# A four-layer residual stack on one core: the set-up work behind the RNN's first 64 steps, laid out anew

## The reference

```python
x = x + L0(x, h0=cond)        # RNN: h = tanh(x_t @ Wx + b + h @ Wh), 1024 steps
x = x + L1(x, conv_w=cond)    # 4-tap convolution, @ Wp and @ Ws, softplus, tanh, state scan, @ Wo
x = x + L2(x, h0=cond)        # LSTM, 512 wide, 1024 steps
x = x + L3(x, ada_emb=cond)   # x @ (base + x_a x_b^T), a matrix of its own for each of the 4 samples

# in L3
h   = gelu(layernorm(ada_emb, ln_g, ln_b) @ w1 + b1)   # 4 x 512
xw  = h @ w2 + b2                                      # w2: 512 x 8192
x_a, x_b = split(xw)                                   # each 4 x 512 x 8
layer = base[None] + einsum('bdr,bkr->bdk', x_a, x_b)  # 4 x 512 x 512
# in L1
decay = 1 - softplus(dt_log) * softplus(A_log)
```

## Time and profile before

| | us |
|---|---|
| median of 3 runs | 3890.44 (3889.31 to 3893.95) |
| profiled execution, its own time | 3886.97 |
| its span in the trace | 3885.2 |
| chunk 1 begins | 101.68 |
| chunk 2 begins | 180.07 |

### The profile page before, as it was taken

The page is one execution under the profiler, slowest core; times in us unless marked ns, Lnnn a source line. Parts: engine busy times, 40 slices in busy tenths (PEclk is TensorE's granted clock), DMA queues, the critical chain, the costliest instruction groups (busy, mean ns, idle before and its releaser), DMA issues.

```text
span 3885.2 us, 254820 instructions
## 1 busy us (share of the span) xinstructions
PE 3622.8 (93%) x110596; PEld 3047.6 (78%) x110596; DVE 3254.4 (84%) x19153; ACT 1648.0 (42%) x8244; POOL 775.5 (20%) x3623
## 2 busy tenths in 40 slices
PE   7899999999999999999999999999999999999875
PEld 5688888888888888888888888888888888887654
DVE  6688888888888888888888888888888888888766
ACT  4244444444444444444444444444444444444332
POOL 1122222222222222222222222222222222222111
PEclk9999999999999999999999999999999999999999
DMA  7100000000000000000000000000000000000000
GB/s 278 49 7 7 10 10 10 8 9 7 10 10 10 10 7 7 10 10 10 10 7 7 10 10 10 10 7 8 9 10 10 10 9 8 7 7 7 6 6 8
DMA packets 19111, 63.30 MB, mean 16 GB/s; under 512 B 3958, under 2 KB 4526, under 8 KB 14914
## 3 DMA queue, kind: packets, MB, share of 16 engines
q1 hardware_dynamic: 17692, 46.67, 3.8%
q10 hardware_dynamic: 294, 0.33, 0.0%
HBM read 38.48 MB, written 8.39 MB: 12 GB/s over the span
## 4 chain that ended last, share of the span: by engine, by line
DVE 50%; PE 45%; issue 4%; DMA 1%; ACT 1%; SPq 0%; POOL 0%; ACTq 0%; DVEq 0%; POOLq 0%
PE ps_lstm L1036 34%; DVE lstm_sums L738 18%; DVE ps_lstm L743 8%; DVE lstm_ig_fc L749 5%; DVE rnn_sums L847 5%; DVE lstm_gates_2c L754 5%; PE ps_rnn L1075 3%; DVE lstm_h_parts L778 3%; PE ps_ssm L1117 2%; DVE lstm_h_scaled L771 2%; DVE lstm_h_parts L774 2%; PE ps_lstm_in_b L1117 2%; PE ps_lstm_in_a L1180 1%; DMA layer_plus_2I<-in_L_cond_w 1%; DVE rnn_h_parts L862 0%
## 5 line engine op out<-in xcount | busy, mean ns | idle before, releaser
L1036 PE MATMUL ps_lstm<-lstm_Wh_parts,lstm_h_parts 128*20 128x256 f16 x65472 | 1970.7, 273 | 221.1 <-DVE lstm_h_parts L778 147.6
L1036 PEld LDWEIGHTS ps_lstm<-lstm_Wh_parts,lstm_h_parts 128*20 128x20 f16 x65472 | 1542.4, 91 | 623.5 <-DVE lstm_h_parts L778 469.3
L738 DVE STREAM_TRANSPOSE lstm_sums<-ps_lstm 128x256 f32<-128x256 f32 x2048 | 913.3, 446 | 184.6 <-PE ps_lstm L1036 157.6
L482 ACT ACTIVATE lstm_gates_2c<-ps_lstm 128x32 f32<-128x32 f32 x2048 | 404.0, 197 | 1405.4 <-DVE ps_lstm L743 1405.4
L346 POOL COPY lstm_sums<-lstm_in 128x32 f32<-128x32 f32 x2048 | 423.9, 210 | 1733.1 <-DVE ps_lstm L743 1733.1
L1075 PE MATMUL ps_rnn<-rnn_Wh_parts,rnn_h_parts 128*20 128x128 f16 x32736 | 639.6, 219 | 25.8 <-DVE rnn_h_parts L862 23.4
L1075 PEld LDWEIGHTS ps_rnn<-rnn_Wh_parts,rnn_h_parts 128*20 128x20 f16 x32736 | 545.4, 92 | 68.9 <-DVE rnn_h_parts L862 48.5
L743 DVE TENSOR_REDUCE ps_lstm<-lstm_sums 128x32 f32<-128x96 f32 x2048 | 554.7, 271 | 34.2
L491 ACT ACTIVATE lstm_tanh_c<-lstm_gates_2c 128x8 f32<-128x8 f32 x2048 | 419.3, 205 | 253.4 <-DVE lstm_gates_2c L754 253.4
L774 DVE TENSOR_TENSOR lstm_h_parts<-lstm_o_scaled,lstm_tanh_c 128x8 f16<-128x8 f32 x2048 | 334.5, 163 | 129.3 <-ACT lstm_tanh_c L491 40.4
L487 ACT ACTIVATE lstm_o_scaled<-lstm_gates_2c 128x8 f32<-128x8 f32 x2048 | 427.4, 209 | 32.1
(11 more groups left out here) (186 smaller groups left out, 2658.6 us busy)
## 6 DMA issues: line engine op xcount, KB each, us to landing
layer_plus_2I<-in_L_cond_w SPq DMA_DIRECT2D x16, 1024.0 KB, 6.6
out<-out_rows SPq DMA_DIRECT2D x128, 64.0 KB, 1.7
x_rows<-in_x SPq DMA_DIRECT2D x31, 256.0 KB
lstm_Wx<-in_L_cond_Wh SPq DMA_DIRECT2D x1, 4096.0 KB, 18.0
lstm_Wx<-in_L_cond_Wx SPq DMA_DIRECT2D x1, 4096.0 KB, 13.6
layer_plus_2I<-in_L_cond_Wh SPq DMA_DIRECT2D x1, 1024.0 KB, 9.8
rnn_Wx<-in_L_cond_Wx SPq DMA_DIRECT2D x1, 1024.0 KB, 11.7
lstm_in<-in_L_cond_w SPq DMA_DIRECT2D x1, 1024.0 KB, 10.5
```

The source lines that it names most:

```text
L738: return mark(V.transpose(tr[h][s % 2][:, :, 0:QC], psL[h][:, 0:HW].rearrange("p (g c) -> p g c", c=QC)))
L1036: ins = mm(psL[h][QC * j:QC * j + LO + NB, 0:HW], hls[:, k, :], whl[:, k, h, e, j, :], start=(k == 0 and e == 0), stop=(k == KB - 1 and e ...
```

## The change

It moves pieces of the set-up to other steps, moves one product from TensorE to GpSimd, and cuts the layer products in halves:

1. w1 is loaded behind the LSTM's `Wh`; its product goes from step 1 to step 9, GELU to step 10, the w2 products from steps 5..24 to steps 11..28 (with 22 and 26 left out).
2. `b2` is no longer added by TensorE. SP loads it into a part of w1's buffer after w1's product (four transfers), and GpSimd adds it, after ScalarE's copy, to each quarter.
3. The maximum of the LSTM's `Wh` starts at step 7 (before 5), and with it the split, which now ends in steps 0 to 2 of chunk 1. The SSM's bias product goes from step 9 to step 5.
4. softplus: ScalarE's Exp in step 1 (before 30), VectorE's part in steps 2 to 5 (before steps 31 to 34). An Exp that nobody reads stands in step 12.
5. Each layer block is formed and added in two halves of 256 columns, 32 in all. They stand at steps 5, 10, 11 (two), 12 to 27 of chunk 1, and three each at steps 28 to 31. From the eighth half on, every second one goes to the bank `ps_x`, and a product then waits only for the addition two halves back.

```diff
-W1_STEP = 1
-GELU_STEP = 2
-W2_STEPS = [5 + -(-5 * q // 4) for q in range(W2N)]
-LMAX_STEP = 5
+W1_STEP = 9
+GELU_STEP = 10
+W2_STEPS = [11, 12, 13, 14, 15, 16, 17, 18, 19, 20, 21, 23, 24, 25, 27, 28]
+LMAX_STEP = 7
-CB_STEP = 9
-SSM_PREP_STEP = CT - 1
-LAYER_STEP = CT
+CB_STEP = 5
+AB_EXP_STEP = 1
+SSM_PREP_STEP = AB_EXP_STEP + 1
+EXP_TABLE_STEP = GELU_STEP + 2
+GATE_SCALE_STEP = CT - 2
+BASE_STEP = CT + 4
+LAYER_STEPS = [CT + s for s in [5, 10, 11, 11] + list(range(12, 28)) + [28] * 3 + [29] * 3 + [30] * 3 + [31] * 3]
+LAYER_W = D // 2
+LAYER_ALT = 6
+        b2q = xl_flat[1].rearrange("p (g n) -> p g n", g=W2G)
+        def layer_bank(v):
+            return psX if v >= LAYER_ALT and v % 2 else psOut
@@ SP
-            sp.dma_start(w1s, rows(w1)).then_inc(d_w1, 16)
...
             sp.dma_start(whl32[:, :, :], rows(l2_Wh)).then_inc(d_lstmw, 16)
+            sp.dma_start(w1s, rows(w1)).then_inc(d_w1, 16)
...
                     sp.wait_ge(rnn_h0_mm, 1)
+                    sp.wait_ge(w1_mm, 1)
+                    for q in range(NQ):
+                        sp.dma_start(b2q[QC * q:QC * q + NB, :, :],
+                                     b2.rearrange("(g q n) -> q g n", q=NQ, n=WQ)[q:q + 1].to_broadcast([NB, W2G, WQ])).then_inc(d_b2, 16)
                     for q in range(W2BUFS - 1, W2N):
@@ GpSimd
+                    if known == 0 and s in W2_STEPS and W2_STEPS.index(s) % KB == KB - 1:
+                        g = W2_STEPS.index(s) // KB
+                        own = xw[:, g // (W2G // 2), :, g % (W2G // 2), :]
+                        if g == 0:
+                            pool.wait_ge(d_b2, 16 * NQ)
+                        pool.wait_ge(xw_raw, g + 1)
+                        Q.tensor_tensor(own, own, b2q[:, g, :].rearrange("p (d r) -> p r d", r=RANK), ALU.add).then_inc(xw_ready, 1)
@@ ScalarE
-            act.dma_start(b2r[:, :], row(b2, WQ)).then_inc(d_b2, 16)
-                                 (psB, psOut)[g % 2][:, 0:WQ].rearrange("p (d r) -> p r d", r=RANK), ACT.Copy).then_inc(xw_ready, 1)
+                                 (psB, psOut)[g % 2][:, 0:WQ].rearrange("p (d r) -> p r d", r=RANK), ACT.Copy).then_inc(xw_raw, 1)
+                    if known in (0, 1) and LSPLIT_STEP <= CT * known + s < LSPLIT_STEP + KB * G:
+                        lstm_weights(CT * known + s - LSPLIT_STEP)
+                        if s == EXP_TABLE_STEP:
+                            A.activation(spw[:, 8, :], spw[:, 0, :], ACT.Exp, scale=-1.0)
@@ VectorE
-                if r > LAYER_STEP and (r - LAYER_STEP) % 2 == 1:
-                    u = (r - LAYER_STEP) // 2
-                    vec.wait_ge(layer_mm, u + 1)
-                    V.tensor_tensor(layer[:, u // KB, u % KB, :], psOut[:, :], baseI[:, u % KB, :], ALU.add
+                for v in [v for v, at in enumerate(LAYER_STEPS) if at == r]:
+                    u, own = v // 2, slice(LAYER_W * (v % 2), LAYER_W * (v % 2 + 1))
+                    vec.wait_ge(layer_mm, v + 1)
+                    V.tensor_tensor(layer[:, u // KB, u % KB, own], layer_bank(v)[:, 0:LAYER_W], baseI[:, u % KB, own], ALU.add
@@ TensorE
-                    if k == KB - 1:
-                        for c in range(NQ):
-                            pick = ident[0:W2G * NQ, g * NQ + c:g * NQ + c + 1].to_broadcast([W2G * NQ, QC])
-                            last = mm(out_[QC * c:QC * (c + 1), 0:WQ], pick, b2r[:, :], start=False, stop=True, tile_position=(0, QC * c))
-                if r >= LAYER_STEP and (r - LAYER_STEP) % 2 == 0:
-                    u = (r - LAYER_STEP) // 2
-                    if u == 0:
+                for v in [v for v, at in enumerate(LAYER_STEPS) if at == r]:
+                    u, own = v // 2, slice(LAYER_W * (v % 2), LAYER_W * (v % 2 + 1))
+                    if v == 0:
                         pe.wait_ge(d_xab, 16 * 2 * NQ * NB)
+                        pe.wait_ge(xw_raw, W2G)
+                    if v == LAYER_ALT + 1:
+                        pe.wait_ge(S["x2_ready"], KB)
+                    if v >= 1:
+                        pe.wait_ge(layer_ready, v - 1 if v > LAYER_ALT else v)
                     w_ = xab[:, u // KB, P * (u % KB):P * (u % KB + 1)]
-                    mm(psOut[:, :], w_, xbb[:, u // KB, :], start=True, stop=True).then_inc(layer_mm, 1)
+                    mm(layer_bank(v)[:, 0:LAYER_W], w_, xbb[:, u // KB, own], start=True, stop=True).then_inc(layer_mm, 1)
```

39 lines of the change are left out of this document (18 added, 21 removed).

## The result

The change makes this kernel slower. The changed kernel takes 3902.82 us in the median of its twelve runs, the kernel before, on the same chip, 3892.7; the ratio is 1.0026, with a 95% interval of 1.0018 to 1.0035. Two of the twelve took 4128.80 and 4156.96 us, at a granted clock of 0.86 and 0.84 over the whole run; range (3899.01 to 3909.07) and ratio go by the other ten, whose median is 3901.87. Repeated in a later comparison it gave 1.0025 (1.0016 to 1.0034). The prediction was 3887.8, with a range to 3895: 15.0 us too low (14.1 against the ten), and no change that can be told where there is a slowdown of 9 to 10. Its profiled execution took 3900.7 us (span 3898.9).

What follows compares the result with a forecast made beforehand. The RNN's state chain bounds steps (2.00 us), SP's go chunk 1's start. Chunk 1 begins 1.1 later, chunk 2 2.3 earlier; 0.3 more gives gain 2.6, 3884.4, plus 3.5 to the median: 3887.8. Range 3883 to 3892, widened to 3881 to 3895.

Steps and rivals of the forecast that it cites:

- SP is already the second path to chunk 1: End of chunk 0: before the change, SP's queue and its go were 0.5 us short of deciding chunk 1's start.
- about 10 us that the RNN gains turn into a wait for `go`: End of chunk 0: RNN ready at 93, but SP lets TensorE begin chunk 1 only at 102.8.
- The run of the queue: SP's commands behind w2 block 12, with 32 small transfers: 22.8 us of issuing that cannot shrink.
- Do the loads keep up?: w2 loads in chunk 0: 0.5 us of waiting, block 12's product out at 77.1, bounds 76.6 and 78.8.
- the hold: Steps 18, 23, 28 of chunk 0: GpSimd's b2 addition holds VectorE's state operation, 0.7 us each, between 0 and 2.0.
- the clock's 1.5: Start of chunk 1: TensorE's clock low after 10 us idle, costing 1.5 us, bounds 0.5 and 3.
- fuller steps 28 to 31 may keep it up: End of chunk 1: fuller steps may keep TensorE's clock up into chunk 2, gaining 0.3 us.
- (a): Rival: SP does not hold chunk 1 back, chunk 2 begins at 166.5, 13.6 earlier, 3876.5 us; chance 0.10, large part included.
- (b): Rival: chunk 0's w2 stretch runs at TensorE's low clock, 8 us through SP in full, 3896 us; chance 0.12.
- (c): Rival: GpSimd's b2 addition far longer than 2.56 us; at 6 us, 3890.5; chance 0.06, shared with another wait in chunk 1.

Runs made afterwards that it cites:

- e2: The changed kernel with SP's release of chunk 1 moved ahead of the 32 small transfers; median 6.5 us above the kernel before.
- e7: The changed kernel loading only half of each w2 block, read twice; steps 10 to 23 took 32.1 us in place of 35.4.
- e11: The changed kernel with GpSimd adding b2 to only an eighth of the columns; step 24 took 2.10 us in place of 3.29.
- e4: The changed kernel with three unread matmuls ahead of the third half in chunk 1's steps 28 to 31; these took 3.97, 5.28, 5.69 and 5.70 us.
- e8: e2 with chunk 1's halves spread, six in place of twelve in steps 28 to 31, and unread matmuls there; median 4.2 us below the kernel before.
- e14: e12 with the maximum's products ahead of most unread matmuls, one half in chunk 1's step 5, and unread matmuls in steps 4 and 5; profiled span 3890.0 us.
- e18: e14 run once more, word for word; 3882.05 us, 0.997 of the kernel before (0.996 to 0.998).
- e12: e8 with the first maximum on TensorE, w1's product in step 7, GELU in 8, w2's blocks respread and its third block asked for early; 3886.2 us.
- e1: The changed kernel with one GpSimd addition of zeros ahead of the partition reduction; the stall stayed, 7.38 us.
- e5: The changed kernel with one GpSimd addition of zeros right behind the partition reduction; that addition took the stall, 9.96 us.
- e6: The changed kernel with 64 one-element GpSimd memsets ahead of the partition reduction; the stall stayed with the piece of x1, 7.48 us.
- e3: The changed kernel with w2's third block asked for ahead of the wait for w1's product; base's load issued at 83.84 us, 0.8 later.

## Why the prediction was wrong, point by point

**The bound and the go: right.** "SP is already the second path to chunk 1" and "about 10 us that the RNN gains turn into a wait for `go`" came true: 8.26 us on TensorE, 12.26 on GpSimd, line 318 as the releaser; e2 removes it. The run of the queue from block 12 on was put at 25.7 and took 24.3.

**The step that failed first: "Do the loads keep up?"** It took 0.5 us of waiting, with 1.7 more as the bound. The 6.6 us from issue to landing were read from a stretch with four blocks in five steps: before, blocks 1 to 12 were used at one in 2.88 us, as this row shows with the one at 74.68 of the earlier trace rows, eleven blocks on:

```profile
43.02 1.02 PE L981 MATMUL ps_lstm_in_b<-layer_plus_2I,hmT 128*32 128x512 f32 x8
```

From 46.0 to 75.6 the DMA engines were busy there for 0.92 of the time already, so that there was little room for a higher rate. The change asks for a block in each of eleven steps of 2.3, and the fastest landing, 4.9, pulled the choice down. With three buffers and a block in every step, a block landed 7.3 us (median) after its issue, the DMA engines moved one MB per 2.85 us, and block 12 came at 82.6, beyond the bound of 78.8. e7 puts the loads at 3.3 to 4.0 us.

**A stall that was not in the prediction: 1.9 us.** 7.42 us of "issue" on GpSimd stood in the trace of before, hidden by a wait for a block. The change moved that wait away, and the prediction, which has no term for GpSimd in this stretch, put the stall at nothing without a reason. With the low clock behind it step 9 began 3.1 us later than put (42.57 against 39.5). w1's product gave 1.15 back: it was costed with a row from a low clock, 1.93, and took 1.05. From step 10 on the loads and the holds added 3.6. So block 12 came 5.5 us late, the queue was 1.4 shorter, chunk 1 began 4.1 late (106.91 against 102.8).

**b2 on GpSimd.** The addition was put at 1.4 and took 1.51 to 1.54; the hold at 0.7 in each of three steps and took 0.9 to 1.3 beyond the operation's own time. The prediction says that two of the holds lie ahead of block 12, but its sum has only one of them there (four steps of 2.0 from 67.1 to 75.1). The trace agrees with the sum: the second met the state at 81.80, behind the start of block 12's product at 81.54. In e11, without most of the addition, block 12 came no earlier: the loads had hidden the first.

**Chunk 1: put at 74.95 with the clock's 1.5, took 80.40.** Steps 0 to 11 took 29.3 (put at 28.65, step 11 3.83 as put at 3.8), steps 12 to 27 36.3 (put at 34.9: a half product takes 0.69 in the rows and not half of 1.12), steps 28 to 31 14.8 (put at 11.4). The last is the second step that failed: "fuller steps 28 to 31 may keep it up". The clock of these steps was full in the count and half in the run, as it had been at the same place before (1.04 for 32 matmuls at 180.07), in steps with less work in them. e4 shows that more matmuls behind the wait don't mend it; e8 shows that fewer halves, matmuls of 128 rows and no wait for an addition together do, in five of six profiles. What brings the clock down stays open: in the changed kernel and in e4 a wait of 0.8 us goes ahead of it, in e14 none does.

**The sum.** Loads, holds and stall +5.5, the queue -1.4, chunk 1 +5.45: chunk 2 at 187.31 against 177.75 put. The first step of chunk 2 adds 1.5 (5.96; the prediction had given it 0.3 less than the 4.76 of before). These 11.1 us are most of the 14; the rest is open. **Rivals.** (a), the whole gain, comes nearest in e18, where SP no longer holds chunk 1 back and much else is changed (chunk 2 at 170.42 against 166.5); (b), slower through the w2 stretch, had the right place and end (block 12 beyond 79.7, a longer stretch that passes through SP in full) and a price of 8 where 3.6 came, but the wrong mechanism: TensorE's clock was 1.00 from 47.0 to 82.6, and the DMA engines, busy for 0.98 of it, were the bound. It was given 0.12. (c) did not occur.

## What to carry to other kernels

Where a queue's last command starts the next stage, take everything that the next stage doesn't need at once out from ahead of it: here what the RNN's steps gained turned into 8.26 us of waiting until that was done. A load that is asked for when a buffer comes free is priced by the buffers' number and the bytes that the DMA engines move, not by the fastest landing in a quieter stretch; spread such loads over all steps that there are (e12: an earlier start, ten waits down to two). And read idle time with no releaser ("issue") as a cost that only seems free as long as another wait lies over it.

## What the runs showed of the hardware that had not been expected

- Behind GpSimd's partition reduction the next two-input addition waits 7.1 to 10 us, once; copies in between don't (e1, e5, e6).
- TensorE's clock stayed at 0.50 while the engine was recorded as busy for 4.00 of 4 us in three windows (176 to 188), and in e14 it fell with no idle time ahead of it. In steps 12 to 27 of the changed kernel, with an equal busy time, it was 1.00. What ran differs: eight matmuls of 128x128 for each step there, only the RNN's 32 with 20 columns and thin ones of 8 rows in the changed kernel's last steps; but e14's had matmuls of 128x128 too, so this alone does not decide it.
- The same program has executions with and without a low clock at the same step, behind a wait of about 1 us (step 11). It cost up to 10.7 us (e3), and the changed kernel's runs span 10 and 14 us.
